# VectorE's work placed between a slot's two maxima, GpSimd's normalisation pulled forward, and expert tiles fetched at loaded addresses

## The chip, the core and the metric

The kernel runs on one core of a Trainium2 chip. The metric is the device time of one execution in microseconds (us). The engines are TensorE (PE, its weight loads shown as PEld), VectorE (DVE), ScalarE (ACT), GpSimd (POOL) and SyncE (SP, which here only issues DMAs); each works through its own queue in order, and they meet through semaphores.

## The reference, cut to what matters

Eight sequences (b) of 512 tokens and 128 channels go through two layers. Both layers have 16-head attention with heads of 8 channels beside a feed-forward part, and both parts read the same normalised input:

```
x  = x + attn0(norm(x)) + ffn0(norm(x))     # ffn0: operands rounded to 4 bits in blocks of 16
xn = norm(x)
x  = x + attn1(xn) + moe(xn)                # shared expert, and 2 of 8 experts per token

gates = softmax(relu(xn @ Wr1 + br1) @ Wr2 + br2)
tg, ti = top_k(gates, 2);  tg = softmax(tg / 2)
out = silu(xn @ Ws1 + bs1) @ Ws2 + bs2
for e in range(8):
    out += sum(tg * (ti == e)) * (silu(xn @ We1[e] + be1[e]) @ We2[e] + be2[e])
```

## The kernel before, in words

**Slots.** The work of a sequence is cut into slots, 16 to a turn. `turn_a(b)` holds the layer-0 scores of sequence b and the layer-1 row maxima of sequence b-1; `turn_b(b)` holds the layer-1 scores of b-1 and the layer-0 maxima of b+1. In a slot PE makes two score pairs E (`score_pair`, L363), four matmuls for the maxima of the next pass (`maxima`, L332), and the weighted sums of the slot before (`weighted_sums`, L351). ACT takes the exponentials of both score pairs (L701), and DVE reduces the maxima's two banks (L987, twice 1.2 us). E and maxima share three double banks of PSUM in turn.

**Other work** (projections, feed-forward, router, the shared expert, normalisation) is put into the slots by hand: every engine has functions `work_a(b, k, place)` and `work_b(b, k, place)` that say what it does in slot k at place "a" (after the first score pair), "b" (after the second) or, on DVE, "c" (after both maxima). Most of it goes through a single PSUM bank, the ring: a product into it waits until the reader of the product before has freed it. So the tables of all engines name the same order.

**The steps named below.** `norm0(b+1)` (PE, slot 0 of turn A, place b) transposes the normalised input of the next sequence, which POOL's `normalize(0, b+1)` writes (L1343, L1352) from the statistics of DVE's `norm_stats` (L885 to L890). `max_rows` (L256, reading nm) transposes 8 heads' maxima; ACT and DVE split them in two bf16 parts (L711, L992) and SP writes them as rows into the score operands (`load_rows`). `q0`, `k0` (L261) and `v0`, `v1` (L266) are projections; `sums_transposed` (L377) and DVE's `sums_divided` (L998, L1000) end a pass of attention. `quantize_x` and `quantize_h` (DVE, L915 to L934) and POOL's `round_x`, `round_h` (L1379, L1382) round to 4 bits; `split_first`, `split_second` (L897 to L903) and POOL's `third_part` (L1370) split queries and keys in three bf16 parts. POOL runs its steps in one fixed order per sequence, without slots.

**Experts.** POOL scatters the normalised tokens of every sequence, row by row, into `xsort`, sorted by expert (`scatter`, L1398). After the last router, DVE computes a table of 39 tiles of 256 tokens (`tile_table`). For each tile POOL gathers weights (526 KB, L1404) and tokens (L1411) with indirect DMAs; `tile_step(i)` on PE transposes tile i+1 (T, L445), makes the hidden layer of tile i (L453) and the output of tile i-1 (L462); DVE copies T and output out of the ring (L1138, L1143), and SP writes the output to `ysort` in tile order (L1613). Tile steps 0 to 15 stand in the slots of `turn_a(8)`, which also hold the last sequence's layer-1 maxima; 16 to 39 follow. Then come the last 16 slots of layer-1 scores, while POOL gathers each token's two results from `ysort` (L1419, 64 indirect DMAs), and DVE's `combine(b)` weights and adds them (L1163). DVE's order has `combine(0)` to `combine(6)` ahead of the last `sums_divided`.

**The start.** `xsort` (16.8 MB) is cleared by 16 DMAs of 1 MB from SP (L1571), ahead of the first `load_rows`.

## Time and profile before

| | us |
|---|---|
| median of 3 runs (lowest, highest) | 1624.69 (1619.58, 1626.31) |
| the profiled execution | 1621.52 |
| its span, first to last instruction | 1619.1 |
| PE busy / DVE / ACT / POOL | 1174.5 / 958.4 / 774.4 / 477.9 |
| DVE's reductions of maxima, 512 of 1217 ns | 601.3 |

No engine is busy all the time: PE has 73% of the span. The program has five stages: a start (to about 101 us), `turn_a(0)` and `turn_b(0)` with half of the slot work missing, the steady turns of sequences 1 to 7 (about 160 us a sequence, to about 1279), the expert tiles (to about 1523) and the last attention pass with the combining. A wait is read in its stage: "idle before" names the time for which an engine stood still and what ended it.

### The profile page before, as it was taken

How to read it: one execution, taken by the hardware profiler on the slowest of the kernel's cores; microseconds unless marked ns; L12 is line 12 of the kernel's file. 1: busy time of each engine (PE TensorE's matmuls, PEld its weight loads, DVE VectorE, ACT ScalarE, POOL GpSimd, SP SyncE). 2: the span in 40 equal slices, each digit the busy share in tenths (PEclk: the TensorE clock that was granted, in tenths of full speed). 3: DMA queues.
4: the chain of work that ended last, by engine and by line, in shares of the span. 5: the costliest groups of instructions: out<-in, count | busy, mean ns of one | idle time of the engine just before them, and what ended most of it. 6: DMA issues, size and time to landing. Idle time of an engine off the chain costs nothing.

```text
span 1619.1 us, 18732 instructions
## 1 busy us (share of the span) xinstructions
PE 1174.5 (73%) x6739; PEld 514.3 (32%) x6807; DVE 958.4 (59%) x1492; ACT 774.4 (48%) x979; POOL 477.9 (30%) x467
## 2 busy tenths in 40 slices
PE   2667578867886788678867986698789468888841
PEld 1113123312331233123312421243124156677510
DVE  7755776767676767676767666766763335311122
ACT  1044164646474547464746474657466423233540
POOL 6041214131313031313131313121131334355475
PEclk9768688989898889898989898989889889999985
DMA  5944252144214421441144114411410464355332
GB/s 136 344 176 111 84 126 69 31 113 110 62 31 115 108 62 31 118 119 48 31 114 123 48 31 122 113 49 25 136 28 1 130 151 130 113 162 172 100 104 70
DMA packets 143230, 159.64 MB, mean 99 GB/s; under 512 B 14586, under 2 KB 132547, under 8 KB 141091
## 3 DMA queue, kind: packets, MB, share of 16 engines
q1 hardware_dynamic: 129986, 123.87, 27.6%
q0 software_dynamic: 12208, 34.04, 7.0%
q8 instruction: 54, 0.88, 0.2%
q10 hardware_dynamic: 944, 0.54, 0.1%
q14 instruction: 38, 0.30, 0.1%
HBM read 90.11 MB, written 67.76 MB: 98 GB/s over the span
## 4 chain that ended last, share of the span: by engine, by line
PE 39%; DVE 23%; ACT 12%; POOL 9%; issue 7%; DVEq 5%; DMA 5%; SPq 0%; ACTq 0%; POOLq 0%
DVE nm L987 12%; PE sums L351 8%; PE mx L363 8%; ACT ex L701 6%; PE mx L332 4%; PE ring L462 3%; PE ring L261 2%; PE ring L437 2%; PE ring L256 2%; DMA ks<-xsort,x_idx 2%; PE mx L453 2%; POOL qs L1419 2%; DVEq L964 2%; PE ring L266 2%; ACT L701 1%
## 5 line engine op out<-in xcount | busy, mean ns | idle before, releaser
L987 DVE TENSOR_REDUCE nm<-mx 128x2 f32<-128x1024 f32 x512 | 601.3, 1217 | 193.9 <-PE mx L332 192.2
L701 ACT ACTIVATE ex<-mx 128x1024 f32<-128x1024 f32 x512 | 514.1, 1024 | 358.8 <-PE mx L363 357.1
L363 PE MATMUL mx<-qs,ks 74*128 74x512 bf16 (+1 forms) x956 | 307.7, 411 | 87.5 <-DVE nm L987 56.1
L351 PE MATMUL sums<-ex,vs 128*18 128x512 f32 x2048 | 295.4, 651 | 5.1 <-ACT pv_sb L705 3.4
L332 PE MATMUL mx<-km,qm 32*128 32x512 bf16 x1024 | 146.0, 426 | 71.3 <-DVE nm L987 48.1
L363 PEld LDWEIGHTS mx<-qs,ks 128*128 128x128 bf16 (+1 forms) x1024 | 77.3, 101 | 366.1 <-issue 167.3
L1370 POOL TENSOR_TENSOR parts<-qk_f,parts 128x512 bf16<-128x512 f32 x32 | 37.2, 1182 | 438.6 <-DVE parts L903 438.6
L1379 POOL TENSOR_TENSOR h_sb<-h_sb,binade 128x704 f32<-128x704 f32 x32 | 53.5, 1670 | 189.8 <-DVE binade L934 188.6
L332 PEld LDWEIGHTS mx<-km,qm 32*128 32x128 bf16 x1024 | 35.1, 93 | 228.1 <-DVE nm L987 92.2
L1343 POOL TENSOR_TENSOR rstd<-veps,minus_half 128x4 f32<-128x4 f32 x16 | 16.6, 1035 | 251.0 <-DVE veps L890 250.9
L1398 POOL DMA_INDIRECT xsort<-xn,pos_i x64 | 62.5, 977 | 35.4 <-DVE pos_i L1071 18.3
L701 ACT ACT_TABLE_LOAD x29 | 37.2, 1283 | 67.5 <-PE mx L363 67.5
L351 PEld LDWEIGHTS sums<-ex,vs 128*18 128x18 f32 x2048 | 35.2, 98 | 81.9 <-issue 63.2
L377 PE MATMUL ring<-ident,pv_sb 128*128 128x128 f32 x128 | 20.8, 287 | 44.5 <-DVE att L1000 42.5
L256 PE MATMUL ring<-ident,xn 128*128 128x128 f32 x64 | 15.1, 381 | 45.8 <-POOL xn L1352 43.7
L256 PE MATMUL ring<-ident,nm 128*8 128x128 f32 x128 | 21.0, 290 | 34.8 <-issue 33.6
L992 DVE TENSOR_TENSOR nm_hl<-ring,nm_hl 8x512 bf16<-8x512 f32 x32 | 21.7, 679 | 41.3 <-ACT nm_hl L711 41.3
L728 ACT ACTIVATE work<-mx,qs 128x256 f32<-128x256 f32 x40 | 15.7, 474 | 60.8 <-PE mx L453 60.8
L1411 POOL DMA_INDIRECT qs<-xsort,x_idx x40 | 37.8, 944 | 14.0 <-issue 8.5
L413 PE MATMUL mx<-xnT,w_sb 128*128 128x512 f32 x64 | 35.7, 685 | 6.8 <-DVE nm L987 6.8
L1143 DVE COPY ks<-ring 128x256 f32<-128x256 f32 x19 | 8.1, 425 | 54.9 <-PE ring L462 54.9
L1143 DVE COPY qs<-ring 128x256 f32<-128x256 f32 x20 | 8.5, 425 | 53.8 <-PE ring L462 53.8
(209 smaller groups left out, 1663.7 us busy)
## 6 DMA issues: line engine op xcount, KB each, us to landing
scratch<-parts SPq DMA_DIRECT2D x128, 256.0 KB, 3.5
ks<-scratch SPq DMA_DIRECT2D x64, 256.0 KB
qs<-scratch SPq DMA_DIRECT2D x64, 256.0 KB
xsort<-hs SPq DMA_DIRECT2D x16, 1024.0 KB, 23.3
qm<-scratch SPq DMA_DIRECT2D x64, 128.0 KB, 2.6
km<-scratch SPq DMA_DIRECT2D x64, 128.0 KB, 2.6
rest<-parts SPq DMA_DIRECT2D x32, 128.0 KB, 3.3
ysort<-qs SPq DMA_DIRECT2D x20, 128.0 KB, 1.8
```

Source lines behind the costliest of these rows:

```text
L256: done = pe.transpose(bank[0:cols, t * P:(t + 1) * P], src(t), ident[:, :])
L332: done = pe.matmul(bank[:, j, :], qm[l][r, g, t * P:(t + 1) * P], km[l][r, g, :], start=True, stop=True)
L351: done = pe.matmul(acc[32 * j:32 * j + 2 * VW, :], values[:, start:start + 2 * VW], ex[:, s % NEX, j, :], start=q == 0 and t == 0, stop=q ...
L363: done = pe.matmul(bank[:, j, :], ks[l][r, h, t * P:(t + 1) * P], qs[l][r, h, :], start=True, stop=True)
L413: done = pe.matmul(bank[:, j, :], w1_sb[:, c * P:(c + 1) * P], xnT[1][:, :], start=True, stop=True)
L462: done = pe.matmul(bank[:, h * P:(h + 1) * P], hm[i % 2][:, c, h * P:(h + 1) * P], wbuf[i % NW][:, FE + c * P:FE + (c + 1) * P], start=c = ...
L701: act.activation(ex[:, s % NEX, 2 * i:2 * i + 2, :], bank[:, :, :], ACT.Exp, scale=SCALE).then_inc(free, 1)
L987: dve.tensor_reduce(nm[l][:, t, h:h + 2], bank[:, :, :], AX.X, ALU.max, negate=True).then_inc(free, 1)
L1370: done = pool.tensor_tensor(parts[:, 2, m, :], qk_f[:, m, :], parts[:, 1, m, :], ALU.subtract)
L1379: pool.tensor_tensor(d, d, binade[:, 0:n], op).then_inc(rounded, 1)
L1398: pool.indirect_dma_start(out=xsort[:, :], out_offset=bass.IndirectOffsetOnAxis(ap=pos_i[:, b, c, t:t + 1], axis=0), in_=xn[1][:, t, :], i ...
L1411: pool.indirect_dma_start(out=xg[i % 2][:, h * P:(h + 1) * P], out_offset=None, in_=xsort[:, :], in_offset=bass.IndirectOffsetOnAxis(ap=x_ ...
```

## The change

**Places.** DVE's slot gets a place "m" between its two maxima, and its longer steps are cut: `norm_stats` / `norm_moments`, `split_first` / `split_second` / `split_third`, `quantize_maxima` / `quantize_scales` / `quantize_scaled` / `quantize_binades`, `router_choice` / `router_hits`. The tables of PE, ACT and DVE are shifted: second-half `max_rows` from slot 0 to slot 1, `v1` and `v0` to place b of slot 1, `q0` to slot 2 and the layer-1 sums to slots 3 and 4, `quantize_h(b, 1)` from slots 1 and 7 to slots 5 to 7, `quantized_x` from slot 6 to slot 0, the gate and up products one slot or so earlier.

```diff
                 if b <= LAST:
-                    if at == (0, "a"):
+                    if at == (1, "a"):
                         max_rows(0, b, 1)
-                    if at == (1, "c"):
+                    if at == (5, "c"):
                         quantize_h(b, 1, 0)
...
                 for k in range(SLOTS):
                     work_a(b, k, "a")
                     work_a(b, k, "b")
                     if b >= 1:
-                        maxima(1, b - 1, k)
+                        maxima(1, b - 1, k, 0)
+                    work_a(b, k, "m")
+                    if b >= 1:
+                        maxima(1, b - 1, k, 1)
                     work_a(b, k, "c")
-                    if b > LAST:
-                        tile_step(k)
+                    if b > LAST and k >= FIRST_TILE:
+                        tile_step(k - FIRST_TILE)
```

On PE, the start of a steady turn A reads before (L256 with nm is `max_rows`, with xn `norm0`; L266 `v1`, the L261 `q0`):

```order
L363 MATMUL mx<-qs,ks 128x512 x2
L256 MATMUL ring<-ident,nm 8x128 x4
L363 MATMUL mx<-qs,ks 128x512 x2
L256 MATMUL ring<-ident,xn 128x128 x4
L332 MATMUL mx<-km,qm 128x512 x4
L351 MATMUL sums<-ex,vs 18x512 x4
L363 MATMUL mx<-qs,ks 128x512 x2
L266 MATMUL ring<-wv_sb,xnT 128x128 x4
L363 MATMUL mx<-qs,ks 128x512 x2
L261 MATMUL ring<-xnT,wqkv_sb 128x512
```

and in the changed kernel (its lines are 8 higher here):

```order
L371 MATMUL mx<-qs,ks 128x512 x4
L264 MATMUL ring<-ident,xn 128x128 x4
L340 MATMUL mx<-km,qm 128x512 x4
L359 MATMUL sums<-ex,vs 18x512 x4
L371 MATMUL mx<-qs,ks 128x512 x2
L264 MATMUL ring<-ident,nm 8x128 x4
L371 MATMUL mx<-qs,ks 128x512 x2
L274 MATMUL ring<-wv_sb,xnT 128x128 x4
L340 MATMUL mx<-km,qm 128x512 x4
L359 MATMUL sums<-ex,vs 18x512 x4
```

The transposes of the maxima have moved behind slot 0's maxima and sums, and `q0` has left slot 1.

**POOL's order.** `normalize(0, b+2)` and `residual0(b+2)` move ahead of `third_part(1, b)` and `round_h(b+1, 0)`. In POOL's queue, from `round_x` of one sequence on, before:

```order
L1379 TENSOR_TENSOR xq<-xq,binade 128x512 x2
L1382 TENSOR_TENSOR xq<-xq,qsc 128x512
L1343 TENSOR_TENSOR rstd<-veps,minus_half 128x4
L1352 TENSOR_SCALAR xn<-x,mv,rstd 128x128 x4
L1364 TENSOR_TENSOR macc<-x,bo_sb 128x512
L1370 TENSOR_TENSOR parts<-qk_f,parts 128x512 x2
L1379 TENSOR_TENSOR h_sb<-h_sb,binade 128x704 x2
L1382 TENSOR_TENSOR h_sb<-h_sb,qsc 128x704
L1343 TENSOR_TENSOR rstd<-veps,minus_half 128x4
L1352 TENSOR_SCALAR xn<-x_sb,mv,rstd 128x128 x4
L1358 TENSOR_TENSOR acc<-x_sb,bo_sb 128x512
```

and after:

```order
L1440 TENSOR_TENSOR xq<-xq,binade 128x512 x2
L1443 TENSOR_TENSOR xq<-xq,qsc 128x512
L1402 TENSOR_TENSOR rstd<-veps,minus_half 128x4
L1411 TENSOR_SCALAR xn<-token 128x4
L1413 TENSOR_SCALAR xn<-x,mv,rstd 128x128 x4
L1425 TENSOR_TENSOR macc<-x,bo_sb 128x512
L1402 TENSOR_TENSOR rstd<-veps,minus_half 128x4
L1413 TENSOR_SCALAR xn<-x_sb,mv,rstd 128x128 x4
L1419 TENSOR_TENSOR acc<-x_sb,bo_sb 128x512
L1431 TENSOR_TENSOR parts<-qk_f,parts 128x512 x2
L1440 TENSOR_TENSOR h_sb<-h_sb,binade 128x704 x2
```

The normalisation of the next layer-0 input (xn from x_sb) now stands directly behind that of layer 1, and the last split and the rounding of h come after it.

**Tiles.** Rows of `xsort` carry the token's number and its first expert behind the 128 channels (XW = 130). SP reads a tile's address from the table into a register and fetches tokens and weights with plain DMAs, the weights one tile ahead; DVE works out from the two extra columns to which row of `y2` each result goes, and POOL scatters the results there with two indirect DMAs a tile. The tile steps start in slot 6 of `turn_a(8)` instead of slot 0.

```diff
+            def fetch_weights(i):
+                first = sp.value_load(w_row[0:1, i:i + 1], min_val=0, max_val=(E - 1) * P)
+                if i >= NW:
+                    sp.wait_ge(ring_full, ring.at(("TO", i - NW))[1] + 1)
+                sp.dma_start(wbuf[i % NW], wmoe[bass.ds(first, P), :]).then_inc(w_in[i % NW], 16)
+
+            def fetch_tokens(i):
+                first = sp.value_load(x_row[0:1, i:i + 1], min_val=0, max_val=ROWS - TS)
+                if i >= 2:
+                    sp.wait_ge(ring_full, ring.at(("T", i - 2))[1] + 1)
+                    sp.wait_ge(y_row_ready, i - 1)
+                sp.dma_start(xg[i % 2], xsort[bass.ds(first, TS), :].rearrange("(h p) c -> p h c", p=P)).then_inc(xg_in[i % 2], 16)
...
+            store_base(LAST - 1)
+            sp.wait_ge(tiles_ready, 1)
+            sp.wait_ge(scattered, 16 * 8 * B)
+            fetch_weights(0)
             for i in range(NTILE):
                 if i == 4:
-                    store_base(LAST - 1)
-                if i == 8:
                     load_rows(1, LAST, 0)
-                if i == SLOTS - 1:
+                if i == 12:
                     load_rows(1, LAST, 1)
-                ring_read(sp, ("TO", i))
-                sp.dma_start(ysort[i * TS:(i + 1) * TS, :].rearrange("(h p) c -> p h c", p=P),
-                             yo[i % 2].rearrange("p (h c) -> p h c", c=P)).then_inc(y_out[i % 2], 16)
+                fetch_tokens(i)
+                if i + 1 < NTILE:
+                    fetch_weights(i + 1)
+            sp.wait_ge(y_out[0], 32 * ((NTILE + 1) // 2))
+            sp.wait_ge(y_out[1], 32 * (NTILE // 2))
             for b in range(B):
+                if b >= 2:
+                    sp.wait_ge(summed, b - 1)
+                for c in range(2):
+                    first = c * PLANE + 1 + b * T
+                    sp.dma_start(yb[b % 2][:, c, :, :], y2[first:first + T, :].rearrange("(t p) c -> p t c", p=P)).then_inc(yb_in[b % 2], 16)
                 if b < LAST:
...
+            def scatter_results(i):
+                pool.wait_ge(y_row_ready, i + 1)
+                ring_read(pool, ("TO", i))
+                for h in range(2):
+                    pool.indirect_dma_start(out=y2[:, :], out_offset=bass.IndirectOffsetOnAxis(ap=y_row[:, i, h:h + 1], axis=0),
+                                            in_=yo[i % 2][:, h * P:(h + 1) * P], in_offset=None).then_inc(y_out[i % 2], 16)
...
             def tile_in(i):
+
                 bank = from_ring(("T", i))
                 dve.tensor_copy(xgT[i % 2], bank[:, 0:TS]).then_inc(ring_free, 1)
+                dve.tensor_scalar(plane[i % 2][:, :], xg[i % 2][:, :, P + 1], t_exp[:, i:i + 1], float(PLANE), ALU.not_equal, ALU.mult)
+                dve.scalar_tensor_tensor(no_token[i % 2][:, :], xg[i % 2][:, :, P], 0.0, aside[:, i, :], ALU.is_equal, ALU.mult)
+                dve.drain()
+                dve.tensor_tensor(plane[i % 2][:, :], plane[i % 2][:, :], xg[i % 2][:, :, P], ALU.add)
+                dve.drain()
+                dve.tensor_tensor(y_row[:, i, :], plane[i % 2][:, :], no_token[i % 2][:, :], ALU.add).then_inc(y_row_ready, 1)
```

**Results.** `y2` holds every token's two results at the token's own place, so that SP reads a sequence's results with two plain DMAs of 256 KB; POOL's 64 gathers are gone, and so is `result_rows` on DVE.

**Clearing.** The 16 DMAs of 1 MB on SP become 32 DMAs of 532 KB that ACT issues, one at the end of each slot of `turn_a(0)` and `turn_b(0)`.

## Rows read from the trace of the kernel before

**Rows 1.** Windows, one steady sequence: us, busy PE, PEld, DVE, ACT, POOL, clock, DMA.

```profile
508.20:538.30 30.10, 17.93 (x84) 6.46 (x80) 14.48 (x19) 10.03 (x13) 10.07 (x9) 0.72 0.65 158
538.30:603.40 65.10, 54.30 (x319) 21.91 (x325) 45.85 (x75) 36.48 (x43) 18.39 (x16) 0.90 0.29 84
603.40:670.00 66.60, 53.26 (x321) 18.18 (x322) 49.67 (x68) 43.36 (x48) 7.66 (x8) 0.97 0.15 39
```

**Rows 2.** Timeline of PE, slots 0 to 2 of one turn A: start, us, work.

```profile
511.17 0.60 PE L256 MATMUL ring<-ident,nm 128*8 128x128 f32 x4 [2.40 <-issue]
...
518.03 1.11 PE L256 MATMUL ring<-ident,xn 128*128 128x128 f32 x4 [5.83 <-POOL xn L1352]
...
531.47 2.08 PE L261 MATMUL ring<-xnT,wqkv_sb 128*128 128x512 f32 x2 [3.00 <-DVE att L1000]
```

**Rows 3.** Timeline of POOL, the same turn and the next turn B.

```profile
514.84 3.13 POOL L1352 TENSOR_SCALAR xn<-x_sb,mv,rstd 128x128 f32<-128x128 f32 x4
...
661.97 2.26 POOL L1370 TENSOR_TENSOR parts<-qk_f,parts 128x512 bf16<-128x512 f32 x2 [32.12 <-DVE parts L903]
```

**Rows 4.** Timeline of DVE, the same two turns.

```profile
528.57 0.89 DVE L915 TENSOR_REDUCE amax<-h_sb 128x44 f32<-128x704 f32 x1
...
635.14 0.17 DVE L890 TENSOR_SCALAR veps<-mv 128x4 f32<-128x4 f32 x1
```

**Rows 5.** Waits of PE for POOL, whole run: us, times, longest.

```profile
PE ring L256 <- POOL xn L1352: 43.7, 7, 10.0
```

**Rows 6.** Timeline of ACT, DVE and PE at the end.

```profile
1558.75 0.59 ACT L705 COPY pv_sb<-sums 128x512 f32<-128x512 f32 x1 [1.17 <-PE sums L351]
...
1597.11 2.35 DVE L1163 SCALAR_TENSOR_TENSOR qs<-qs,tg 128x128 f32<-128x128 f32 x8 [7.68 <-DMA qs<-ysort,y_idx]
...
1600.28 0.71 PEld L377 LDWEIGHTS ring<-ident,pv_sb 128*128 128x128 f32 x4 [40.48 <-DVE att L1000]
```

**Rows 7.** Windows, expert tiles: wait for tile 0; slots with maxima; tiles alone.

```profile
1279.60:1303.30 23.70, 1.09 (x7) 0.40 (x7) 4.71 (x9) 0.00 (x0) 13.38 (x15) 0.53 0.93 224
1303.30:1407.80 104.50, 85.64 (x541) 67.05 (x542) 50.29 (x69) 29.22 (x71) 41.80 (x45) 0.98 0.42 129
1407.80:1522.70 114.90, 94.42 (x617) 85.01 (x618) 19.79 (x46) 36.62 (x93) 59.06 (x63) 0.99 0.49 149
```

**Rows 8.** Timeline of PE, two transposes of tiles one step apart.

```profile
1493.98 0.44 PE L445 MATMUL ring<-ident,qs 128*128 128x128 f32 x2 [1.64 <-DMA qs<-xsort,x_idx]
...
1498.54 0.41 PE L445 MATMUL ring<-ident,ks 128*128 128x128 f32 x2 [0.61 <-DVE qs L1143]
```

**Rows 9.** Timeline of PE and ACT's queue, the start.

```profile
3.23 1.42 ACTq L834 DMA_DIRECT2D work<-w_up  x3
...
96.27 1.01 PE L363 MATMUL mx<-qs,ks 74*128 74x512 bf16 x2 [6.68 <-DMA qs<-nm_hl]
...
101.09 1.09 PE L256 MATMUL ring<-ident,xn 128*128 128x128 f32 x4 [2.10 <-DVE nm_hl L992]
```

**Rows 10.** Windows, the clearing and turn A of sequence 0.

```profile
57.00:101.00 44.00, 20.16 (x67) 4.87 (x65) 37.24 (x45) 4.20 (x5) 10.11 (x9) 0.54 0.85 358
101.00:142.00 41.00, 38.64 (x229) 13.01 (x232) 11.38 (x18) 32.73 (x38) 11.50 (x8) 0.93 0.44 120
```

**Rows 11.** The page's costliest groups: the maxima's reductions, count, busy us, mean ns.

```profile
L987 DVE TENSOR_REDUCE nm<-mx 128x2 f32<-128x1024 f32 x512 | 601.3, 1217 | 193.9 <-PE mx L332 192.2 <-issue 0.4
```

**Rows 12.** Timeline of SP's queue, its last issue of the score operands.

```profile
1297.75 3.27 SPq L1531 DMA_DIRECT2D qs<-rest  x1
```

**Rows 13.** DMA issues: count, KB each, median us to landing.

```profile
qs<-base SPq DMA_DIRECT2D x4, 256.0 KB, 3.0
out<-qs SPq DMA_DIRECT2D x4, 256.0 KB, 2.4
...
qs<-ysort,y_idx POOLq DMA_INDIRECT x32, 2.5
...
qs<-wmoe,w_idx POOLq DMA_INDIRECT x20, 4.6
```

More of the change, by code:

```diff
@@ L35 @@
 ROWS = E * CAP
-NZERO = ROWS // (16 * P)
+XW = P + 2
+ZR = 8
+NZERO = ROWS // (ZR * P)
+PLANE = B * T + 1
+FIRST_TILE = 6
 TS = 256
@@ L87, in two_layers @@
 def two_layers(nc, x, w_qkv, w_out0, b_out0, w_gate, w_up, w_down, wqT, wkT, wvT, woT, bq, bk, bv, bo,
-               wr1, br1, wr2, br2, w1s, b1s, w2s, wmoe, b2, scratch, rest, xsort, ysort, base, out):
+               wr1, br1, wr2, br2, w1s, b1s, w2s, wmoe, b2, scratch, rest, xsort, y2, base, out):
     ctx = ExitStack()
@@ L518, in work_b @@
                 at = (k, place)
-                if b >= 1 and at == (0, "a"):
+                if b >= 1 and at == (1, "a"):
                     max_rows(1, b - 1, 1)
@@ L639, in _ @@
             turn_a(B)
-            for i in range(SLOTS, NTILE + 1):
-                if i == SLOTS:
+            for i in range(SLOTS - FIRST_TILE, NTILE + 1):
+                if i == SLOTS - FIRST_TILE:
                     max_rows(1, LAST, 1)
@@ L854, in _ @@
             turn_a(B)
-            for i in range(SLOTS, NTILE):
-                if i == SLOTS:
+            for i in range(SLOTS - FIRST_TILE, NTILE):
+                if i == SLOTS - FIRST_TILE:
                     max_rows(1, LAST, 1)
@@ L953, in quantize_x @@
                     dve.drain()
-                    quantize_scales(src, T, qsc[0])
+                    quantize_maxima(src, T)
                 if step == 1:
-                    wait(dve, h_ready, 2 * b)
-                    quantize_binades(dst, src, T).then_inc(xq_scaled, 1)
+                    quantize_scales(T, qsc[0])
+                if step == 2:
+                    quantize_scaled(dst, src, T)
+                if step == 3:
+                    quantize_binades(dst, T).then_inc(xq_scaled, 1)
             def quantize_h(b, i, step):
@@ L980, in ffn_down, with maxima @@
                 dve.tensor_tensor(a, a, bank[:, :], ALU.add).then_inc(ring_free, 1)
-            def maxima(l, b, u):
+            def maxima(l, b, u, i):
                 g, t = u // NT, u % NT
-                for i in range(2):
-                    bank, free = from_pair(("M", l, b, u, i))
-                    h = 4 * g + 2 * i
-                    dve.tensor_reduce(nm[l][:, t, h:h + 2], bank[:, :, :], AX.X, ALU.max, negate=True).then_inc(free, 1)
+                bank, free = from_pair(("M", l, b, u, i))
+                h = 4 * g + 2 * i
+                dve.tensor_reduce(nm[l][:, t, h:h + 2], bank[:, :, :], AX.X, ALU.max, negate=True).then_inc(free, 1)
             def max_rows(l, b, half):
@@ L1116, in tile_table @@
[L1116 removed]
+                dve.tensor_scalar(t_row[:, :], t_row[:, :], float(TS), None, ALU.mult)
                 dve.drain()
[L1118 removed]
+                dve.scalar_tensor_tensor(t_row[:, :], t_exp[:, :], float(CAP), t_row[:, :], ALU.mult, ALU.add)
                 dve.drain()
[L1120 removed]
@@ L1270, in turn_b @@
                     if b + 1 <= LAST:
-                        maxima(0, b + 1, k)
+                        maxima(0, b + 1, k, 0)
+                    work_b(b, k, "m")
+                    if b + 1 <= LAST:
+                        maxima(0, b + 1, k, 1)
                     work_b(b, k, "c")
@@ L1305, in _ @@
             quantize_weights(2)
-            for step in range(2):
+            for step in range(4):
                 quantize_x(0, step)
@@ L1314, in _ @@
                     max_rows(0, 0, 0)
-                maxima(0, 0, u)
+                for i in range(2):
+                    maxima(0, 0, u, i)
                 if u == 12:
                     quantize_h(0, 0, 0)
+                    quantize_h(0, 0, 1)
                 if u == 13:
-                    quantize_h(0, 0, 1)
+                    quantize_h(0, 0, 2)
+                    quantize_h(0, 0, 3)
                 if u == 14:
                     norm_stats(0, 1)
+                    norm_moments(0, 1)
             dve.wait_ge(weights_in, 16 * N_WEIGHT_DMAS)
@@ L1326, in _ @@
             turn_a(B)
-            for i in range(SLOTS, NTILE + 1):
-                if i == SLOTS:
+            for i in range(SLOTS - FIRST_TILE, NTILE + 1):
+                if i == SLOTS - FIRST_TILE:
                     max_rows(1, LAST, 1)
@@ L1464, in _ @@
                 residual1(b)
+                if b + 2 <= LAST:
+                    normalize(0, b + 2)
+                    residual0(b + 2)
                 third_part(1, b)
```

306 lines of the change are left out of this document (154 added, 152 removed).

## The prediction

> **What bounds the kernel now.** I read first the page's busy shares, which name no engine, then the windows by stage, then in each stage the longest waits and the timeline around them.
>
> In a steady sequence [rows 1] the first three slots of turn A take 30.1 us although PE has 17.9 us of work in them, and that at a granted clock of 0.72; DVE has 14.5. The rest of turn A is 65.1 us with PE busy 54.3, turn B 66.6 us with 53.3. So two stretches are near PE's own work and one is a hole. The timeline says what the hole is [rows 2]: PE waits 2.40 us at the maxima's transposes, because DVE has not finished the last reductions, then 5.83 us for POOL's xn, and 3.00 us at `k0`, whose place in the ring is held until DVE has divided the sums. POOL writes that xn at 514.84 [rows 3], while the statistics of the same step come from DVE in turn B (635.14 is the next sequence's [rows 4]) and POOL then stands idle for 32.12 us until the split at 661.97 [rows 3]: the normalisation is late by its place in POOL's queue alone. The third wait stems from DVE: at 528.57 it begins `quantize_h`'s first step (amax) in slot 1 [rows 4], ahead of the division. The waits for POOL sum to 43.7 us, 7 times [rows 5]; 10.0 of it is the program's first wait, so six turns have 33.7, or 5.6 each.
>
> After the tiles PE is through with the last scores when ACT's copy ends at 1558.75 + 0.59 = 1559.3, but cannot go on until 1600.28, 40.48 us later [rows 6]: in DVE's queue the last division stands behind `combine(0)` to `combine(6)`, and those wait for POOL's gathers (7.68 us before the last). Of the tile stage, the 24 steps without maxima take 114.9 us with PE busy 94.4 [rows 7]; a step that no fetch holds takes 1498.54 - 1493.98 = 4.56 us, one whose tokens are late up to 1.64 more on its start [rows 8]. PE bounds this stage and POOL's fetches are just behind it (63 issues, 59.1 us).
>
> **The change, part by part**, against the profiled execution (1621.52, span 1619.1 and 2.4 around it; the median of the runs is 3.2 above it).
>
> *Start and sequence 0.* SP's queue is freed of the 16.8 MB, so the wait of 6.68 us for the row load at 96.27 [rows 9] goes. What is late next is `norm0(1)`: it ran at 101.09, and POOL's normalisation in the start, which isn't moved, ends near 97; so 4 us of 6.68 are gained. Against that, ACT issues one clearing DMA per slot: three took 1.42 us [rows 9], so 0.47 each, 16 x 0.47 = 7.6 us if nothing hides them in turn A of sequence 0, where ACT is busy 32.7 of 41.0 us [rows 10]; nothing if its sequencer runs ahead of the running exponential. I take 3. Turn B of that sequence has no exponentials and hides them. Net -1, bounds -6.7 and +7.6. The clearing itself ran at 358 GB/s [rows 10]; 16 pieces of 0.53 MB are 24 us of such traffic beside a DMA share of 0.44 of 41 us (18 us): the queues are full in this turn, but the first load that must land, the maxima's operands for turn B, has the latter two thirds of the turn for it. The Trainium skill (DMA: Bandwidth & Descriptors, Issuing engines are not separate DMA queues) says that DMAs issued by any engine interleave on the same 16 DMA engines and that a second issuer saves only issue time; by that rule ACT's queue adds no bandwidth, and the sum above, which adds the two shares, is the right one.
>
> *Slots 0 to 2 of turn A, sequences 1 to 6.* `normalize(0, b+2)` now follows layer 1's and has the 32 us of idle POOL; `max_rows` stands in slot 1, after DVE's reductions; `quantize_h` stands in slots 5 to 7. All three waits go. What is left: PE's 17.9 us at clock 0.72 are 17.9 x 0.72 / 0.95 = 13.6 at the later stretches' clock; DVE's 14.5. New in slots 1 and 2 are two ring waits: `v1` behind the transposes, ACT's cast and DVE's subtraction (about 1.2 us after cover by a score pair), and `k0` behind ACT's copy (0.5). I take 18 us instead of 30.1, so -12 x 6 = -72. Bounds: only POOL's wait goes, -34; down to DVE's work, (30.1 - 14.5) x 6 = -94.
>
> *Rest of turn A.* The pieces on both sides of the second maximum add no DVE work; they let the first bank free before the long piece. PE idles 65.1 - 54.3 = 10.8 us here, but much of that is the shared expert's table loads on ACT and the router's chain. I take a seventh, -1.5 x 6 = -9, and -3 for the last turn A, which has the wait at the transposes but no `norm0`. Bounds 0 and half the idle time, -32.
>
> *Turn B, sequences 1 to 6.* PE idles 13.3 us of 66.6; DVE is busy 49.7. The products move one slot earlier, and the splitting and rounding at its end get interleaved; but DVE's own total stays, and `v0` now stands behind `max_rows` in the ring. I take -3 x 6 = -18, bounds +12 (2 us of ring wait in each) and -40 (half the idle time).
>
> *Tiles.* Before, PE waits for tile 0 until 1303.3, busy 1.1 us of 23.7 [rows 7]. Now six slots of maxima fit in there (six pairs of reductions are 12 x 1.22 = 15 us [rows 11]). But SP issues its last score operand at 1297.75 and is blocked on it 3.27 us [rows 12], so tile 0's fetch starts at about 1301; two register loads, two issues and 3 to 4.6 us to landing [rows 13] bring it to 1308, and step 0 ends near 1313, 6 later than before. Then 9 slots with maxima at 104.5 / 15 = 7.0 us and 30 steps at 4.56, 137: 1513. SP's `load_rows` at tiles 4 and 12 hold the token fetch behind them until the maxima's rows exist; I add 6 us for both: 1519, against 1522.7, so -4. DVE's five short operations a tile run while PE makes the output product. What is queued behind a register load on SP is every later fetch: if two loads and two issues pass 4.56 us, SP sets the step. No row shows such a load; SP's nearest are issues (0.47 as ACT's above) and the shortest landing of a 256 KB transfer (2.4 [rows 13]). With 0.47 for the load a tile costs SP 1.9 us and nothing is lost; with 2.4, 5.7 us, (5.7 - 4.56) x 39 = +45. I take 1 us, near the issue, since it is a word and not a tile: 2.9 us, hidden. The Trainium skill gives a floor of about 600 ns for a tensor_load (DMA: Bandwidth & Descriptors, Latency and other measured facts); by that it would be 2.1 us a tile, hidden as well; no run here has shown one. Bounds -12 (no stall at the rows) and +45.
>
> *The end.* Let X be the last tile's copy, 1522.7 before. Two scatters at 0.94 (59.06 / 63 [rows 7]) and 2.5 us to landing, then a result load of 3 to 4, then `combine`, 2.35 [rows 6]: the first ends at X + 11 to 12. From there one buffer pair takes store 2.4, base load 3.0 [rows 13] and combine 2.35, 7.75 us for every second sequence: six more end at X + 11.5 + 6 x 3.9 = X + 35. PE's last sums are copied at X + 36.6, as before. So both arrive together, X + 38 with some collision, instead of 1599.5 = X + 76.8: -38. The chain of 19.6 us from there to the end of the span stays. Bounds -25 (a base load twice as long) and -40.2 (PE alone).
>
> Sum: -1 - 72 - 12 - 18 - 4 - 38 = -145, so 1621.5 - 145 = 1476.5, say 1476.
>
> **The rivals.**
> *The slots keep their length.* POOL's wait goes, but the single ring and DVE fill slots 0 to 2; elsewhere the pieces win nothing. For it: turn B is already 80% PE, and DVE's work is the same. Against: three separate waits end in that hole. Then -1 - 34 - 4 - 38 = -77: 1544.
> *The slots close up.* DVE's work in pieces frees both banks in time, slots 0 to 2 fall to 14.5 and half of the other idle time goes: -4 - 94 - 32 - 40 - 4 - 40 = -214: 1408. For it: most of PE's short waits in turn B are for a bank after a long DVE step. Against: ACT's table loads and the ring stay.
> *SP becomes the bound of the tiles, and it gets slower.* Place: the two register loads a tile, in SP's one queue ahead of both fetches. If each takes as long as a weight fetch takes to land (4.6 us [rows 13]) the step is 2 x (4.6 + 0.47) = 10.1 us, 5.6 more than PE's, x 39 = +218, less the -141 of the other parts: about 1699. It shows from a load of 1.8 us up, and eats the whole gain at 3.6. Against: nothing else in the kernel waits so for one word.
> *The fetch at loaded addresses changes nothing* is inside the forecast: the tile stage is PE's, and its term is -4.
>
> **How the numbers follow.** The forecast has 0.56, the slots that keep their length 0.20, those that close up 0.19, SP as the bound 0.05. The likeliest one's own range is 1440 to 1515 (its terms off by a third). The range to be given reaches most of the way to both slot rivals: 1418 to 1545. Less than 0.5% (8 us) is what a measurement of this kernel can't tell from no change. The first three cases are all faster; SP as the bound is slower for loads above 3.6 us and faster below. Faster 0.95, same 0.02, slower 0.03.
>
> **What would show it.** In turn A, no PE wait for POOL's xn from sequence 1 on, slots 0 to 2 near 18 us at a clock above 0.9, and a sequence of 145 us instead of 162. At the start, PE's first score pair near 90 (96.27 - 6.68) and `norm0` near 97. Tile steps of 4.5 to 4.6 us with PE's wait for tokens gone, except at tiles 4 and 12, and tile 0 near 1308 less what the turns gave. At the end, PE's wait for the division a few us instead of 40. It is wrong if the sequences keep 155 us or more, if SP's loads stand between the tiles, or if the results' loads end later than PE.

## The result, and the profile after

The changed kernel takes 1533.33 us (median of 4 runs, 1527.91 to 1541.76) against 1625.43 before: ratio 0.9445, 95% interval 0.9397 to 0.9494. The forecast was 1476. So the change gained 92 us where 145 were forecast.

The profiled execution of after took 1541.76 (span 1540.0), the slowest of its four, so its trace shows 79 us of gain. First the steady sequence of [rows 1] again, cut where PE starts the first score pair of turn A, of its slot 3, of turn B and of the next turn A (windows: from:to, length, busy PE, PEld, DVE, ACT, POOL, granted clock, DMA share, GB/s):

```profile
502.70:517.80 15.10, 13.26 (x72) 4.68 (x68) 7.46 (x8) 8.40 (x11) 1.39 (x1) 0.85 0.72 177
517.80:584.40 66.60, 54.93 (x334) 23.09 (x335) 49.41 (x86) 37.62 (x44) 18.45 (x16) 0.90 0.38 99
584.40:656.60 72.20, 55.58 (x320) 17.77 (x320) 52.17 (x71) 43.29 (x48) 16.68 (x17) 0.94 0.17 45
```

The first window of [rows 1] doesn't end at such a pair: 538.30 is where PE starts the router's product in slot 3, 2.4 us after that slot's first score pair. Cut at the pair, turn A of before reads

```profile
508.17:535.86 27.69, 16.02 (x76) 5.53 (x73) 13.11 (x18) 8.73 (x11) 10.07 (x9) 0.71 0.71 172
535.86:603.37 67.51, 56.21 (x331) 22.84 (x332) 47.22 (x78) 37.79 (x44) 18.39 (x16) 0.89 0.28 81
```

So slots 0 to 2 fell from 27.7 to 15.1 us, a gain of 12.6 where 12 were forecast. To the router's product, which is what the forecast's 18 us end at, they fell from 30.1 to 17.4 (before, then after):

```profile
538.31 1.04 PE L261 MATMUL ring<-xnT,wr_sb 128*32 128x512 f32 x2 [0.52 <-DVE att L1000]
...
520.15 1.04 PE L269 MATMUL ring<-xnT,wr_sb 128*32 128x512 f32 x2 [0.81 <-DVE att L1031]
```

The rest of turn A is 0.9 us shorter, and turn B, where 3 us of gain were forecast, 5.6 us longer. The sequence is 153.9 us, not 145. Summed over the run, between the first exponentials of the turns (turn B of sequence 0, which has none, from its first maxima; the last line from the last attention's first exponential to the end):

| stretch | forecast, us | trace, us |
|---|---|---|
| start up to turn B of sequence 0 | -1 | -1.0 |
| turn B of sequence 0 | no term but the clearing, hidden | +4.5 |
| slots 0 to 2 of turn A, sequences 1 to 6 | -72 | -65.2 |
| rest of turn A, and the last turn A | -12 | -8.3 |
| turn B, sequences 1 to 6 | -18 | +29.7 |
| tiles (with the last turn B, which had no term) | -4 | -1.5 |
| end | -38 | -37.5 |

One line carries most of the miss, 48 of 66 us. PE's waits over the whole run (us, times, longest), first lines of before that stand beside [rows 5], then after:

```profile
PE mx L363 <- DVE nm L987: 56.1, 41, 2.9
PE mx L332 <- DVE nm L987: 48.1, 77, 2.7
...
PE ring L256 <- issue: 33.6, 27, 3.2
```

```profile
PE mx L340 <- DVE nm L1018: 84.0, 78, 2.7
...
PE mx L421 <- DVE nm L1018: 20.1, 14, 1.6
PE mx L371 <- DVE nm L1018: 19.7, 34, 2.7
PE ring L274 <- DVE nm_hl L1023: 19.2, 13, 1.5
PE ring L264 <- DVE nm_hl L1023: 16.2, 7, 3.6
...
PE ring L264 <- POOL xn L1413: 12.1, 2, 9.9
```

POOL's wait is gone but for two in the start, 9.9 and 2.2 us. The 33.6 us in which the maxima's transposes waited (the profile names no releaser; at the first wait of [rows 2] VectorE's last reductions end 0.1 us ahead of them) became 35.4 behind those transposes, where the ring's next user waits for VectorE's subtraction (nm_hl): an exchange. And the waits for a bank that VectorE has not reduced yet (nm, all lines that name it) rose from 119.6 to 140.8 us. Turn B cut in two, slots 0 to 10 and 11 to 15 (windows, first before, then after):

```profile
603.40:650.60 47.20, 39.69 (x238) 14.97 (x236) 32.52 (x49) 33.45 (x38) 5.40 (x6) 0.96 0.11 26
650.60:670.00 19.40, 13.57 (x87) 3.21 (x86) 17.14 (x20) 9.91 (x10) 2.26 (x2) 1.00 0.25 71
```

```profile
584.40:633.90 49.50, 40.09 (x239) 14.57 (x238) 32.93 (x49) 33.52 (x38) 11.07 (x13) 0.97 0.11 25
633.90:656.60 22.70, 15.49 (x86) 3.21 (x84) 19.24 (x23) 9.77 (x10) 5.62 (x4) 0.87 0.30 89
```

The first part grew by 2.3 us, 1.54 of them the wait behind `max_rows` in slot 1. The last five slots grew by 3.3: PE idles 1.4 longer, and its work takes 1.9 longer at a granted clock of 0.87 instead of 1.00. VectorE, third of the busy times, is busy 88% and 85% of these slots. PE's timeline there, in the turn B ahead (start, duration; in brackets the wait and what ended it), and VectorE's beside it:

```profile
487.32 0.40 PE L340 MATMUL mx<-km,qm 32*128 32x512 bf16 x4 [1.22 <-DVE nm L1018]
...
491.60 0.39 PE L340 MATMUL mx<-km,qm 32*128 32x512 bf16 x4 [1.31 <-DVE nm L1018]
...
495.90 0.40 PE L340 MATMUL mx<-km,qm 32*128 32x512 bf16 x4 [1.57 <-DVE nm L1018]
...
500.38 0.58 PE L340 MATMUL mx<-km,qm 32*128 32x512 bf16 x4 [1.75 <-DVE nm L1018]
```

```profile
487.27 1.23 DVE L921 TENSOR_TENSOR qk_f<-qk_f,parts 128x1024 f32<-128x1024 f32 x1
488.41 1.22 DVE L1018 TENSOR_REDUCE nm<-mx 128x2 f32<-128x1024 f32 x1
489.72 0.69 DVE L925 CAST parts<-qk_f 128x1024 bf16<-128x1024 f32 x1
490.33 1.22 DVE L1018 TENSOR_REDUCE nm<-mx 128x2 f32<-128x1024 f32 x1
491.65 0.89 DVE L936 TENSOR_REDUCE amax<-h_sb 128x44 f32<-128x704 f32 x1
```

A reduction, then pieces, then a reduction, without a hole from 484.2 to 500.3: eight reductions and all pieces, 16 us (the two reductions of the last slot follow 0.7 us later). Before, the same work ran from 654.5 to 670.6, 16 us as well. What differs is who waits: before, PE's first score pair of turn A started at 669.97, ahead of the last piece's end, and PE paid in slot 0, at the transposes and under the wait for xn [rows 2], in which VectorE caught up. After, that hole is closed, and with the pieces between the reductions PE meets the queue in turn B.

The sums of the other stages came out as reckoned. At the start the first score pair and `norm0` (forecast "near 90" and "near 97"):

```profile
90.91 1.01 PE L371 MATMUL mx<-qs,ks 74*128 74x512 bf16 x2 [0.62 <-DVE nm L1018]
...
97.89 1.12 PE L264 MATMUL ring<-ident,xn 128*128 128x128 f32 x4 [2.20 <-POOL xn L1413]
```

The -1 of this stage is right by luck. The first score pair came 5.4 us earlier, but the second then waited 2.74 us for VectorE's reductions and `norm0` 2.20 us for POOL, so that 1.0 us was left of the forecast's 4 when turn B began. And the 3 us booked for ACT's clearing DMAs don't show: slots 3 to 14 of that turn A take 28.7 us before and 28.9 after.

Tile 0 came at 1268.83, the forecast's 1308 less the 40 us that the turns gave, and SP's two issues of a tile show what a register load costs: from 1309.74 to 1310.58, 0.84 us at most (the prediction took 1):

```profile
1268.83 0.69 PE L453 MATMUL ring<-ident,qs 128*128 128x128 f32 x2 [12.32 <-DMA qs<-xsort]
```

```profile
1309.40 0.34 SPq L1585 DMA_DIRECT2D ks<-wmoe  x1
1310.58 0.39 SPq L1592 DMA_DIRECT2D ks<-xsort  x1
```

At the end, where [rows 6] had a wait of 40.48 us, PE waits 4.73. The first and the seventh `combine` end 11.9 and 39.1 us behind the last tile's copy (1481.6), against 11 to 12 and 35:

```profile
1491.16 2.35 DVE L1183 SCALAR_TENSOR_TENSOR qs<-qs,tg 128x128 f32<-128x128 f32 x8 [9.56 <-DMA qs<-base]
...
1518.32 2.35 DVE L1183 SCALAR_TENSOR_TENSOR qs<-qs,tg 128x128 f32<-128x128 f32 x8 [2.76 <-DMA qs<-base]
```

```profile
1521.50 1.11 PE L385 MATMUL ring<-ident,pv_sb 128*128 128x128 f32 x4 [4.73 <-DVE att L1031]
```

### The profile page after: what moved, and what is told of

It reads as the page before. It is cut to its first block, busy times and chain, and to the rows that moved or that the text cites. A ratio compares the mean times of both kernels' runs of the same rounds, so it can differ in the third digit from the quotient of the medians.

```text
span 1540.0 us, 19413 instructions
## 1 busy us (share of the span) xinstructions
PE 1173.6 (76%) x6739; PEld 514.9 (33%) x6807; DVE 973.6 (63%) x1651; ACT 770.5 (50%) x979; POOL 384.6 (25%) x373
## 4 chain that ended last, share of the span: by engine, by line
PE 44%; DVE 24%; ACT 9%; DVEq 9%; issue 5%; DMA 4%; SPq 2%; POOL 1%; ACTq 0%; POOLq 0%
DVE nm L1018 12%; PE sums L359 9%; PE mx L371 7%; ACT ex L709 5%; PE mx L340 5%; PE ring L470 4%; PE mx L461 3%; PE ring L269 2%; PE mx L421 2%; PE ring L445 2%; PE ring L274 2%; PE ring L264 2%; DVEq L993 2%; PE ring L327 1%; ACT L709 1%
## 5 line engine op out<-in xcount | busy, mean ns | idle before, releaser
L1018 DVE TENSOR_REDUCE nm<-mx 128x2 f32<-128x1024 f32 x512 | 608.3, 1217 | 182.1 <-PE mx L340 181.0
L709 ACT ACT_TABLE_LOAD x29 | 37.2, 1283 | 65.2 <-PE mx L371 65.2
L1466 POOL DMA_INDIRECT y<-qs,y_row x40 | 38.4, 960 | 108.9 <-DVE qs L1163 101.6
L421 PE MATMUL mx<-xnT,w_sb 128*128 128x512 f32 x64 | 36.0, 691 | 20.1 <-DVE nm L1018 20.1
L1466 POOL DMA_INDIRECT y<-ks,y_row x38 | 36.5, 959 | 56.1 <-DVE ks L1163 50.3
L445 PE MATMUL ring<-w_sb,hs 128*128 128x128 f32 x256 | 36.3, 285 | 0.6 <-DVE ks L1163 0.6
L306 PE MATMUL mx<-wgT,xqT 128*128 128x352 f32 x64 | 26.8, 551 | 12.9 <-DVE nm L1018 12.8
```

What stands on the lines that cost most here:

```text
L421: done = pe.matmul(bank[:, j, :], w1_sb[:, c * P:(c + 1) * P], xnT[1][:, :], start=True, stop=True)
L445: pe.matmul(bank[:, t * P:(t + 1) * P], hs[:, c, t * P:(t + 1) * P], w2_sb[:, c, :], start=c == 0, stop=False)
L709: act.activation(ex[:, s % NEX, 2 * i:2 * i + 2, :], bank[:, :, :], ACT.Exp, scale=SCALE).then_inc(free, 1)
L1018: dve.tensor_reduce(nm[l][:, t, h:h + 2], bank[:, :, :], AX.X, ALU.max, negate=True).then_inc(free, 1)
L1466: pool.indirect_dma_start(out=y2[:, :], out_offset=bass.IndirectOffsetOnAxis(ap=y_row[:, i, h:h + 1], axis=0), in_=yo[i % 2][:, h * P:(h + ...
```

## The experiments

The edits below are condensed, and only their main lines are shown. Theory one: the end of turn B is VectorE's queue, and the hole in slot 0 had hidden it. Theory two: the pieces between the reductions cost the time. Two more questions are what POOL's order is worth by itself, and where the rest of PE's waits can be taken out. Ratios are to the kernel before.

| run | median, us | ratio (95%) |
|---|---|---|
| changed kernel | 1533.33 | 0.9445 (0.9397 to 0.9494) |
| `tail_pieces_back` | 1537.13 | 0.9481 (0.9439 to 0.9522) |
| `h0_late` | 1526.22 | 0.9418 (0.9384 to 0.9452) |
| `h0_fill` | 1522.14 | 0.9373 (0.9326 to 0.9421) |
| `pool_back` | 1573.34 | 0.9688 (0.9651 to 0.9725) |
| `before_pool` | 1600.61 | 0.9887 (0.9821 to 0.9952) |
| `x_late` | 1531.76 | 0.9460 (0.9402 to 0.9518) |
| `tile0_early` | 1544.92 | 0.9491 (0.9427 to 0.9555) |
| `rows_end` | 1528.43 | 0.9400 (0.9341 to 0.9459) |
| `best1` | 1496.99 | 0.9214 (0.9185 to 0.9243) |
| `best2` | 1487.92 | 0.9154 (0.9123 to 0.9184) |
| `best3` | 1486.99 | 0.9141 (0.9104 to 0.9178) |
| `best4` | 1489.83 | 0.9176 (0.9138 to 0.9215) |

**tail_pieces_back: the same work in the old places.**

```diff
-if at == (11, "m"): split_first(1, b)
-if at == (11, "c"): split_second(1, b)
-if at == (12, "m"): split_third()
+if at == (11, "c"): split_first(1, b)
+if at == (12, "c"): split_second(1, b); split_third()
-quantize_h(b + 1, 0, ·) at (12, "c"), (13, "m"), (13, "c"), (14, "m")
+quantize_h(b + 1, 0, 0 and 1) at (13, "c"), 2 and 3 at (14, "c")
```

> The changed kernel with the pieces of slots 11 to 14 of turn B back behind both reductions, in the slots of the kernel before (split_first 11, split_second and split_third 12, quantize_h in two halves 13 and 14). Theory one (VectorE's sum of work sets the end of turn B, wherever in the slot it stands): turn B stays within 1.5 us of 72.3, the time within 8 us of 1533. Theory two (the pieces between the reductions are what lengthened turn B): turn B falls back to about 67.5 us, 5 us in each of seven sequences, about 1500 us.

Both theories are half right. The place of the pieces does set the last five slots: 19.2 us at a granted clock of 1.00 in all six turns, as before, and turn B is back at 68.4 to 68.7 in four of them (70.2 and 70.8 in the others). But slots 0 to 2 rose to 16 us, PE meets the queue at turn A's second score pair instead, and the median is the changed kernel's within the intervals. The profiled execution shows 2 us less for the two stretches together (85 instead of 87); the medians don't bear that out.

**h0_late: 3.7 us of VectorE's work out of the end of turn B.**

```diff
-quantize_h(b + 1, 0, ·) in slots 12 to 14 of turn B
+quantize_h(b, 0, 0) at (0, "c"), 1 at (1, "c"), 2 at (2, "m"), 3 at (2, "c") of turn A
```

> The changed kernel with the four pieces of quantize_h(b+1, 0) taken out of slots 12 to 14 of turn B and put into slots 0, 1 and 2 of the next turn A, where VectorE idles 1.3, 2.5 and 3.3 us. Theory one (the end of turn B is VectorE's: ten reductions of 1.22 us and the pieces run there without a gap, 16 us for five slots, and the old wait for xn in slot 0 hid it): slots 11 to 15 fall from 23.1 to about 17.5 us, slots 0 to 2 of turn A rise from 14.7 to about 16, so 4 to 5 us in each of seven sequences: about 1503 us, 0.925 of the kernel before. Theory two (a piece between the two reductions holds up the second bank wherever it stands): the piece in slot 2 costs there what it cost in slots 13 and 14, and the time stays within 8 us of 1533.

The last five slots of turn B fell to 18.8 us, turn B to 68.2 in most sequences, and slots 0 to 2 didn't rise but fell to 13.1: together better than theory one asked (17.5 and 16). Yet the total is 1526, not 1503, and within the intervals the changed kernel's. Slot 3 of turn A rose from 4.6 to 8.3 us: the last piece now stood ahead of the division, and the next user of the ring, the router's first product, behind that. It is a wait like the third of [rows 2], one slot later; there `k0` stood behind the division, here (and in the expectation of `h0_fill`, which names `k0`) it is the router (PE, then VectorE):

```profile
510.45 1.25 PE L269 MATMUL ring<-xnT,wr_sb 128*32 128x512 f32 x2 [3.03 <-DVE att L1031]
```

```profile
508.50 0.53 DVE L958 TENSOR_SCALAR binade<-h_sb 128x704 int32<-128x704 int32 x1
509.10 0.53 DVE L960 TENSOR_SCALAR binade<-binade 128x704 f32<-128x704 f32 x1
509.54 0.35 DVE L1029 RECIPROCAL rden<-ring 128x32 f32<-128x32 f32 x1
```

**h0_fill: the same pieces, where nothing waits behind them.**

```diff
+quantize_h(b, 0, 0) at (0, "c"), 1 at (1, "a"), 2 at (1, "c"), 3 at (3, "b") behind sums_divided
```

> The same move of quantize_h(b, 0) out of the end of turn B as in the kernel with all pieces in slots 0 to 2, but each piece put where VectorE waits and nothing that PE waits for stands behind it: the maxima behind slot 0, the scales between max_rows and values1 in slot 1 (VectorE idle 1.25 us there), the product behind slot 1, the binades behind the first division in slot 3 (idle 1.46 us). Theory one (VectorE's queue at the end of turn B was the loss, and the pieces in slot 2 only gave it back because the division, and with it PE's k0, stood behind them, 3.0 us): turn B stays at 68.2 us, slot 3 of turn A falls from 8.3 back to 4.6, so about 20 us less than with the pieces in slots 0 to 2: 1505 us, 0.930 of before. Rival (VectorE has no free time at the start of turn A either): slots 1 and 2 grow by 1 to 2 us, between 1512 and 1526.

Slots 1 and 2 did not grow, slot 3 fell back to 4.6 us, and slot 4 rose to 8.2 in most turns: neither forecast's place, though the total lies in the rival's range. `split_first`, a cast of 0.68 us, took 1.55 there, the second division stood behind it, and PE waited (VectorE, POOL, PE):

```profile
512.65 1.55 DVE L917 CAST parts<-qk_f 128x1024 bf16<-128x1024 f32 x1
514.12 0.34 DVE L1029 RECIPROCAL rden<-ring 128x32 f32<-128x32 f32 x1
```

```profile
510.22 3.43 POOL L1442 TENSOR_TENSOR h_sb<-h_sb,binade 128x704 f32<-128x704 f32 x2 [22.99 <-DVE binade L960]
```

```profile
515.11 1.25 PE L274 MATMUL ring<-wr_sb,r_sb 32*128 32x8 f32 x6 [2.38 <-DVE att L1031]
```

**pool_back and before_pool: POOL's order alone.** Both exchange the same two blocks, in after and in before:

```diff
 residual1(b)
+if b + 2 <= LAST:
+    normalize(0, b + 2)
+    residual0(b + 2)
 third_part(1, b)
 if b + 1 <= LAST:
     round_h(b + 1, 0)
-if b + 2 <= LAST:
-    normalize(0, b + 2)
-    residual0(b + 2)
```

(shown for `before_pool`; `pool_back` is its reverse.)

> The changed kernel with POOL's normalize(0, b+2) back behind third_part and round_h. By the prediction's price of that wait (33.7 us for six turns) 1567 us. Theory one: xn comes 4.8 + 4.2 us behind the last piece of quantize_h, some 4 us after PE wants it in slot 0, and VectorE uses that hole to work off its queue, so +10 to +25 us, 1543 to 1558. If neither, and the order of POOL is worth nothing with the other edits in place, within 8 us of 1533.

> The kernel before with one edit: POOL's normalize(0, b+2) moved ahead of third_part and round_h, as in the changed kernel. By the price of the wait alone 33.7 us less, 1592 us, turn B unchanged at 67 us, slots 0 to 2 of turn A at about 21 us instead of 26 to 28, since the waits for the last reductions and for the divided sums stay. If VectorE's queue is late anyway (theory one in its strong form), the hole only changes its name: under 15 us gained, above 1610.

Undone in the changed kernel, the order costs 40 us, a little above the prediction's 33.7; theory one's 10 to 25 was too low. The waits for xn are back (8 times, the program's first among them):

```profile
PE ring L264 <- POOL xn L1413: 44.9, 8, 10.0
```

Done alone in the kernel before, it gains 20 us of the 33.7 in the medians (its four runs lie between 1592 and 1612, so the interval is 8 to 29 us): POOL's wait is gone there too, but slots 0 to 2 fell only to 21 to 24 us, since the waits for VectorE stay. So the order of POOL's queue is worth more beside VectorE's new order than without it.

`pool_back` also says what the hole did and what it did not. With the hole open again and the pieces between the reductions, turn B is still 70.7 to 72.3 us; so it is the pieces' place that lengthens turn B. The open hole shortens turn B by at most 1.6 us and adds 5 to 7.5 us to slots 0 to 2.

**x_late, tile0_early, rows_end: three smaller waits.**

```diff
-quantize_x(b + 1, ·) at (11, "c"), (12, "m"), (12, "c"), (13, "m")      # x_late
+quantize_x(b + 1, 0 to 3) at (14, "c")
+fetch_weights(0); fetch_tokens(0); fetch_weights(1)                      # tile0_early
 load_stacks(1, LAST, 0)
-if i == 4: load_rows(1, LAST, 0)                                         # rows_end
+if i == 6: load_rows(1, LAST, 0)
-combine(6); sums_divided(1, LAST, 0); sums_divided(1, LAST, 2)           # rows_end
+sums_divided(1, LAST, 0); sums_divided(1, LAST, 2); combine(6)
```

> The changed kernel with quantize_x(b+1) taken out of slots 11 to 13 of turn A, all four pieces behind slot 14, where VectorE waits 5.0 us for PE's shared_out. Theory one (slots with pieces are VectorE's): slots 12 and 13 fall from 4.2 + 3.8 to about 3.1 + 3.1 us, 1.8 us in each of seven sequences, about 1521 us. Rival: POOL's rounding (3.7 us) then ends behind PE's transposes of xq in slot 0 of turn B, which wait up to 2 us each: 1533 or up to 5 us more.

> The changed kernel with the fetches of tile 0 (weights, tokens) and of tile 1's weights ahead of SP's last 16 stack loads and of store_base, instead of behind them. The chain through SP's queue: tile 0's tokens leave about 12 us earlier, PE's wait of 12.3 us ahead of tile 0 falls to 2 us or less, tile 0 near 1258, about 1523 us in all. Rival: the tokens wait for the last scatter, or the tile stage is held by the stacks that now come later: under 3 us gained.

> The changed kernel with two edits in separate stages. One: SP's load of the first maxima's rows of the last sequence at tile 6 instead of tile 4, so that no fetch stands behind rows which do not exist yet: PE's 7.3 us wait at tile 4 goes, steps 4 to 6 at 5.2 us. Two: combine(6) behind the last division instead of ahead of it: PE's 4.7 us wait for the division falls to about 1, and combine(6) fits into the 4.1 us in which VectorE waits for the last projection. Together 7 + 3.5 us: about 1523. Rivals: the four row issues (2.6 us) hold the fetch at tile 6 just as well (no gain in the tiles); or the end of combine(6) becomes the end of the kernel (no gain there).

`x_late`: slot 13 fell from 3.8 to 3.2 us, slot 12 stayed at 4.2, and turn B of sequence 0 grew by 3.5, since turn A of sequence 0 has no maxima and PE came early for xq. No gain shown. `tile0_early` gained nothing: tile 0 was in time, but PE's queue has tile 1's transposes ahead of tile 0's products, and those tokens now stood behind the stack loads:

```profile
1261.37 0.66 PE L453 MATMUL ring<-ident,qs 128*128 128x128 f32 x2 [0.85 <-DVE macc L1043]
1276.81 0.69 PE L453 MATMUL ring<-ident,ks 128*128 128x128 f32 x2 [14.78 <-DMA ks<-xsort]
```

`rows_end` did in its trace what was forecast: tiles 3 to 10 took 47.4 us instead of 53.7, the stretch from the last attention's first exponential to the end 3.2 less. In the medians that is 5 us and within the intervals.

**best1 to best4: the pieces together.** `best1` has `h0_fill`, `split_first` behind the second division of slot 4, `x_late`, the fetches of tiles 0 and 1 ahead of the last stack loads (which go to tiles 11 and 16), and `rows_end`. `best2` puts both halves of the shared expert's product, and both gate products, into one slot each. `best3` mends `quantize_x` in sequence 0 and spreads the stack loads over tiles 14 to 21. `best4` has `router_hits` one slot earlier.

```diff
-if at == (3, "c"): split_first(0, b + 1)                                 # best1
+if at == (4, "a"): sums_divided(1, b - 2, 2); split_first(0, b + 1)
-if at == (8, "b"): shared_hidden(b - 1, 1)                               # best2
+if at == (7, "b"): shared_hidden(b - 1, 0); shared_hidden(b - 1, 1)
-if i == 11: load_stacks(1, LAST, 0)                                      # best3
-if i == 16: load_stacks(1, LAST, 1)
+if 14 <= i < 22: load_stacks(1, LAST, (i - 14) // 4, (i - 14) % 4)
-if at == (8, "m"): router_hits(b - 1)                                    # best4
+if at == (7, "m"): router_hits(b - 1)
```

> What the runs so far point to, together: quantize_h(b, 0) in VectorE's waits of slots 0 to 3 of turn A; split_first of layer 0 behind the second division of slot 4, so that it no longer stands ahead of it while POOL rounds h (it took 1.55 us there instead of 0.68, and PE waited 2.4 us); quantize_x behind slot 14; tiles 0 and 1 fetched ahead of the last stack loads, those in the tile loop at tiles 11 and 16, the first maxima's rows at tile 6; combine(6) behind the last division. Theory one (VectorE's queue ahead of what PE waits for, and SP's queue ahead of what the tiles wait for): turn A 78.5, turn B 68.2, so 147 a sequence instead of 153 (about -44), PE's wait for tile 0 from 12.3 to about 2 (-10), tile 4 -6, the end -3.5: about 1470 us, 0.907 of before. Rival (a wait removed in one slot comes back in the next, as in the two runs that moved quantize_h): a sequence stays at 150, about 1490 to 1505.

> The same, and both halves of the shared expert's hidden product in slot 7 of turn A (before: slots 7 and 8), both gate products in slot 6 of turn B (before: 6 and 7), so that ScalarE loads its table for them once and not twice (two loads of 1.28 us less in each turn). If ScalarE sets slots 7 and 8 of turn A (15.0 us, ScalarE busy 11.7) and 6 and 7 of turn B (12.6 us, busy 10.6): 2.5 us less in each turn, 5 a sequence, about 35 us less than without it. Rival: PE's products hold two of the three score banks at once, and PE and VectorE wait for them what ScalarE gains: within 8 us of the run without it.

> The version with the table loads halved, and two places mended that its trace shows. In sequence 0, quantize_x goes back behind slot 11 (turn A0 has no maxima, PE came 6.4 us too early for xq): 61.4 us of A0's last slot and turn B0 fall to about 56, -5. The last stack loads go one by one into tiles 14 to 21 instead of eight at tile 16, where step 15 took 11.8 us and step 16 6.4: both back to 4.5 to 5, -8. Together about 1475 us, 0.907 of before. Rival (each of these loads delays the tokens behind it on the same queue, so that spreading them spreads the stall): the tile part stays, about 1483.

> The same, with router_hits one slot earlier (ahead of the second maximum of slot 7), so that its copy and its mask no longer run beside POOL's rounding of h, where they took 1.04 and 1.22 us instead of 0.17 and 0.19. If that collision costs PE time (slots 8 and 9): about 1 to 1.9 us in each of six turns, 6 to 11 us less than without it. Rival: the 1.9 us lie in VectorE's slack, or slot 7 loses what slot 8 gains: within 4 us of it.

`best1` closes the sequences as theory one said, 147.1 us for the three windows that take 153.9 in after:

```profile
493.10:506.20 13.10, 11.21 (x72) 4.22 (x68) 10.41 (x13) 8.29 (x11) 0.00 (x0) 1.00 0.68 205
506.20:571.30 65.10, 54.21 (x339) 22.60 (x335) 50.73 (x88) 37.46 (x44) 22.79 (x19) 0.92 0.45 114
571.30:640.20 68.90, 56.08 (x324) 18.62 (x320) 48.28 (x64) 43.27 (x48) 13.97 (x16) 0.95 0.14 37
```

VectorE's 109 us are the same as in after; 3 to 4 of them went from turn B into slots 0 to 2, where it had idled. What the run misses of its 1470: the turns gave 37 us in the traces and not 44, sequence 0 gained nothing, and the stack loads at tile 16 (a wait of 9.1 us; tiles 9 to 38 took 11 us longer) gave back the 10 us won ahead of tile 0; its forecast was also reckoned from an execution of after that lies 8 us above after's median. `best2` gained 9 us of the 35 expected: slots 6 and 7 of turn B fell from 12.6 to between 10.8 and 12.2, slots 7 and 8 of turn A not at all on average (13.9 to 16.2 us, against 15.0 in `best1`). `best3` mended sequence 0 by 6 us in its trace; the spread loads cost the tiles what the block had cost, as the rival said. Its total is `best2`'s. `best4` gained nothing. It ended the collision of `router_hits` with POOL's rounding, and the router's next two steps, which take 0.16 to 0.17 us each alone, ran into the same rounding and took up to 0.84 and 1.39:

```profile
532.72 1.39 DVE L1076 TENSOR_TENSOR e<-gpair 128x4 f32<-128x4 f32 x1
```

So whether the collision costs PE time stays untested.

## Why the prediction was right in kind and wrong in size

- **Slots 0 to 2.** Right in mechanism and size: a gain of 12.6 us instead of 12 in the steady sequence, 17.4 us instead of 18 to the router's product, and no PE wait for xn after the start. Two readings were off without harm to the sum: the 30.1 us hold 2.4 us of slot 3, and the clock of these slots is 0.85, not above 0.9. The sum, -65 instead of -72, is smaller because sequence 1 had little to lose (20.1 us before).
- **Turn B, the step that failed.** "The products move one slot earlier ... but DVE's own total stays ... I take -3 x 6 = -18, bounds +12 ... and -40" measured +29.7, outside its bounds. The sentence on DVE's total was right, and the conclusion was not drawn: four of the last five slots of turn B hold eight reductions and all the pieces of the split and of half of h, 16 us without a gap, and the hole that the change closes was time in which that was worked off. The interleaving, for which the sum has no cost, moved PE's wait for this queue from slot 0 into turn B. So the two terms belong together: turn B and slots 0 to 2 of the next turn A lost 5.5 to 9 us in a steady sequence, not 15. The runs side by side (us between first exponentials, turns B of sequences 2 to 5 with the slots behind them):

| kernel | turn B | slots 0 to 2 | sum |
|---|---|---|---|
| before: pieces behind both reductions | 66.6 to 67.8 | 25.6 to 28.1 | 93.0 to 95.8 |
| `before_pool`: the hole for POOL closed | 66.4 to 67.7 | 21.0 to 23.6 | 87.6 to 90.0 |
| `pool_back`: pieces between, hole open | 70.7 to 72.3 | 19.2 to 20.8 | 91.4 to 91.8 |
| after: pieces between, hole closed | 71.1 to 73.6 | 13.1 to 14.9 | 84.2 to 87.6 |
| `tail_pieces_back`: pieces behind both, hole closed | 68.4 to 70.8 | 14.6 to 16.3 | 84.3 to 85.4 |
| `h0_late`: 3.7 us of pieces taken out | 68.2 to 70.4 | 13.1 to 13.4 | 81.3 to 83.5 |
| `best1`: the same pieces in VectorE's waits | 68.5 to 68.9 | 13.1 to 13.4 | 81.6 to 82.2 |

  The pieces' place decides in which turn PE waits, and the sum falls when the hole closes and when work leaves this end of turn B. That VectorE caught up in the hole of before is read from the timelines and not tested by a run of its own. In `h0_late` that work held up slot 3 instead; in `best1` it did not, and a sequence takes 146 to 147 us.
- **Turn B of sequence 0** had no term but the hidden clearing, and pays 4.5 us in the same way: in `h0_late`, with the pieces taken out of its end, turns A and B of sequence 0 take 4.0 us less than in after.
- **Start, tiles, end** came within 3 us each, the first two partly by luck: in the start a gain of about 1 instead of 4 met a cost near 0 instead of 3, and of the tiles with maxima four took 5.2 us instead of 7.0, while the rows' stall at tile 4 alone was 7.3 instead of 6 for two.
- **The rivals.** "The slots keep their length" has the nearest time, 1544, but not the mechanism: the slots closed. SP as the bound of the tiles is refuted: most steps without maxima take 4.53 us, as PE's 4.56 of before, and a register load at most 0.84 us. The Trainium skill (DMA: Bandwidth & Descriptors, Latency and other measured facts) gives a floor of about 600 ns for such a load, and the 0.84 us don't contradict it.
- What stays open: how much of turn A's slots 7 and 8 (15.0 us, ScalarE busy 11.7) is ScalarE's, since halving its table loads there gave nothing on average.

## What to carry to other kernels

A hole on one engine is also the time in which another catches up; before its length is booked as gain, add up what the other engines' queues hold at that place. Move work into an engine's waits only when nothing that someone waits for stands behind it in that queue: `h0_late`, `h0_fill` and `tile0_early` turned a removed wait into a new one one slot or tile later. Where the border between two stages can shift, compare their sum.
